# Graph network kernel: column numbers in PSUM for the merges, 30 batches fetched early, scores from folded source products

## The reference, cut to what matters

```
# layer 1 (relations), last step: sum the edge messages by destination, and add them to x
out = segment_sum(msg, dst);  x = x + out
# layer 2: this, twice (first on h = relu(layernorm(x)), then on its own output h1)
q = h @ wq + bq;  k = h @ wk + bk;  v = h @ wv + bv;  e = edge_attr @ we
score = sum(q[dst] * (k[src] + e), -1) / 8
alpha = softmax of score over the edges of one dst
out   = segment_sum(alpha[:, None] * (v[src] + e), dst) + h @ ws + bs
```

## Time and profile before

| | us |
|---|---|
| median of 3 runs | 6880.25 (6879.4 to 6884.29) |
| the profiled execution, its own time | 6867.82 |
| its span in the profile | 6865.4 |
| busy: PE, DVE, ACT, POOL | 4521.3, 4547.4, 1784.2, 3994.9 |
| stretch of rew, from its first hot to its last sum | 2401 to 2744 |
| at1s | 2779 to 3606 |
| at1w | 3642 to 3984 |
| at2s | 4016 to 4826 |
| at2w | 4867 to 5205 |

### The profile page before, as it was taken

The page is one execution under the profiler, slowest core; times in us unless marked ns, Lnnn a source line. Parts: engine busy times, 40 slices in busy tenths (PEclk is TensorE's granted clock), DMA queues, the critical chain, the costliest instruction groups (busy, mean ns, idle before and its releaser), DMA issues. The chain is left out here.

```text
span 6865.4 us, 102108 instructions
## 1 busy us (share of the span) xinstructions
PE 4521.3 (66%) x31726; PEld 4063.2 (59%) x31726; DVE 4547.4 (66%) x5826; ACT 1784.2 (26%) x2462; POOL 3994.9 (58%) x3348
## 2 busy tenths in 40 slices
PE   6665345770188788466766857777587856875897
PEld 3454335660177787466665856766587755764675
DVE  7898553225677788699989833333887965772458
ACT  5543112330044344233323411111343420000001
POOL 0397765771277678777765877775000027757756
PEclk9766668995598999688778979999899978997999
DMA  6498766668855477333335844444477861221109
GB/s 234 108 275 257 154 149 140 141 133 321 339 174 166 136 243 251 78 96 99 101 84 184 265 125 136 131 131 125 149 254 281 312 244 41 56 91 50 14 11 299
DMA packets 865606, 1128.70 MB, mean 164 GB/s; under 512 B 591583, under 2 KB 604276, under 8 KB 864060
## 3 DMA queue, kind: packets, MB, share of 16 engines
q1 hardware_dynamic: 409660, 807.13, 35.3%
q10 hardware_dynamic: 311296, 226.11, 10.8%
q0 software_dynamic: 144256, 90.12, 9.0%
HBM read 633.88 MB, written 495.44 MB: 164 GB/s over the span
## 5 line engine op out<-in xcount | busy, mean ns | idle before, releaser
L895 POOL DMA_INDIRECT gc_msgs<-t,src_rows x784 | 754.4, 962 | 1131.5 <-POOLq L148 837.3
L2005 PEld LDWEIGHTS gc_ring<-gc_msgs,gc_hot 128*128 128x128 f32 x4736 | 621.6, 208 | 310.4 <-issue 303.6
L2005 PE MATMUL gc_ring<-gc_msgs,gc_hot 128*128 x4736 | 648.8, 295 | 234.1 <-SPq L1964 233.0
L949 POOL DMA_INDIRECT acc<-de_sums,de_put x392 | 607.5, 1550 | 307.7 <-issue 146.6
L895 POOL DMA_INDIRECT edge_rows<-x,dst_rows x392 | 508.4, 1297 | 164.9 <-issue 117.1
L895 POOL DMA_INDIRECT edge_rows<-h,dst_rows x392 | 479.5, 1223 | 210.5 <-issue 117.3
L895 POOL DMA_INDIRECT re_rows<-x,src_rows x392 | 406.2, 1036 | 125.3 <-issue 124.7
L895 POOL DMA_INDIRECT at1s_ends<-x,src_rows x392 | 395.6, 1009 | 128.8 <-issue 119.2
L895 POOL DMA_INDIRECT at2s_ends<-h,src_rows x392 | 372.3, 950 | 134.7 <-issue 118.2
L1477 PE MATMUL re_psR<-w_rel,re_own 128*128 128x128 f32 x3136 | 396.9, 292 | 70.9 <-DVE re_own L1414 70.4
L1477 PEld LDWEIGHTS re_psR<-w_rel,re_own 128*128 128x128 f32 x3136 | 389.6, 208 | 80.1 <-issue 77.1
(11 more groups left out here) (491 smaller groups left out, 11718.9 us busy)
## 6 DMA issues: line engine op xcount, KB each, us to landing
rew_win<-x SPq DMA_DIRECT2D x74, 544.0 KB, 4.8
at1w_win<-g SPq DMA_DIRECT2D x74, 544.0 KB
at2w_win<-g SPq DMA_DIRECT2D x74, 544.0 KB, 4.1
de_win<-t ACTq DMA_DIRECT2D x74, 512.0 KB, 4.6
de_near<-same SPq DMA_DIRECT2D x74, 512.0 KB, 5.0
x<-rew_win SPq DMA_DIRECT2D x74, 512.0 KB
h<-at1w_win SPq DMA_DIRECT2D x74, 512.0 KB
h<-at2w_win SPq DMA_DIRECT2D x74, 512.0 KB, 2.9
```

The source lines that it names most:

```text
L895: nc.gpsimd.indirect_dma_start(buf[:, t * width:(t + 1) * width], None, table, bass.IndirectOffsetOnAxis(ap=rows[:, t:t + 1], axis=0)).the ...
L949: nc.gpsimd.indirect_dma_start(g.acc0[j % LANES], bass.IndirectOffsetOnAxis(ap=put[:, j:j + 1], axis=0), sums[:, j * D:(j + 1) * D], None, ...
L2005: done = nc.tensor.matmul(ring[:, bass.ds(to[n], SLOT)], hot[k][:, n, :], each_group(msgs[:, bass.ds(of[n], MID)], SLOT // MID), start=Fal ...
```

## The change

Four edits.

1. In the merges VectorE reads the column numbers from a copy in PSUM (`fixed`, one bank). For that bank the two output buffers, `ring[0:2048]` and `ring[1536:3584]`, now overlap in one bank: the last four steps' slots of a block. The odd block's slots run backwards. ScalarE clears 12 slots of a block early (`clear`) and the four shared ones (`clear_shared`) only once the block before has been summed out; TensorE waits for that ahead of its product 12.
2. `AHEAD` is 30: destination rows of batches 24 to 29 move, 48 gathers each, from at1s into rew and from at2s into at1w. The score stages make 544 gathers.
3. Scores: k and v of an edge and the score's form in the query weights come from one product of width 258 (`psU`, four banks): 128 columns for (k+e) wq^T, 128 for v+e, 2 for bq.(k+e). The biases come in by a row of ones under the transposed attributes. The folded weights are made once per stage (`lay_out` and the first six products of TensorE). Gone are the transposes `psD`, the copy `hdT`, q, k, three bias additions and, in at1s, the scaling of the destination rows by the layernorm's root (eight numbers per partition are scaled instead). `score` is now `dot` (VectorE: max, times, sum), `keep` (ScalarE: v+e and the two columns out of `psU`) and a small sum.
4. The own products of at2s take both weight tables as one of 256 columns (`own_w`): half as many instructions, equal columns.

The diff, cut; in merges the addresses of the products differ to match, and in `setup` a column table for them:

```diff
-AHEAD = 24
+AHEAD = 30
...
+                link(v.tensor_scalar(ahead[:, :], edge[:, :], edge[:, 0:1], None, ALU.subtract))
+                link(v.tensor_tensor(lift[:, :], ahead[:, :], at[:, :], ALU.subtract))
+                link(v.scalar_tensor_tensor(lift[:, :], lift[:, :], odd[:, :], at[:, :], ALU.mult, ALU.add))
+                link(v.tensor_scalar(g.steps[:, 2 * S:3 * S], lift[:, :], float(SLOT), None, ALU.mult))
...
-        ps = [r.ps(f"ps{k}", [P, S * SLOT]) for k in range(2)]
+        ring, fixed = r.ps("ring", [P, RING]), r.ps("fixed", [P, 512])
+        SHARED = 3 * 512
+        MOST = SHARED // SLOT
+        upper = ring[:, SHARED:SHARED + S * SLOT]
+        slots = [grouped(ring[:, 0:S * SLOT], SLOT), grouped(upper, SLOT)[:, ::-1, :]]
...
+                    to = grouped(local[m % 2][:, :], SLOT) if m % 2 else grouped(local[m % 2][:, :], SLOT)[:, ::-1, :]
+                    nc.scalar.activation(to[:, :, 0:D], grouped(msgs[:, bass.ds(first, S * D)], D), ACT.Copy).then_inc(copied, 1)
+
+                def width(m):
+                    return SLOT if m < 2 else D if counts is None else D + 1
 
                 def clear(m):
                     if m >= 2:
                         act.wait_ge(added, m - 1)
-                    width = SLOT if m < 2 else D if counts is None else D + 1
-                    nc.scalar.activation(grouped(ps[m % 2][:, :], SLOT)[:, :, 0:width], each_group(blank[:, 0:width], S), ACT.Copy).then_inc(zeroed, 1)
+                    nc.scalar.activation(slots[m % 2][:, 0:MOST, 0:width(m)], each_group(blank[:, 0:width(m)], MOST), ACT.Copy).then_inc(zeroed, 1)
+
+                def clear_shared(m):
+                    if m >= 1:
+                        act.wait_ge(added, m)
+                    nc.scalar.activation(slots[m % 2][:, MOST:S, 0:width(m)], each_group(blank[:, 0:width(m)], S - MOST), ACT.Copy).then_inc(zeroed_shared, 1)
...
+                copy(0)
+                clear(0)
                 for m in range(BLOCKS):
-                    copy(m)
-                    clear(m)
+                    if m + 1 < BLOCKS:
+                        copy(m + 1)
+                    clear_shared(m)
+                    if m + 1 < BLOCKS:
+                        clear(m + 1)
...
+                        if n == MOST:
+                            pe.wait_ge(zeroed_shared, m + 1)
+                        back = slice((S - 1 - n) * SLOT, S * SLOT)
+                        to, of = (upper[:, back], local[k][:, :]) if k else (ring[:, 0:S * SLOT], local[k][:, back])
+                        done = nc.tensor.matmul(to[:, bass.ds(at[n], SLOT)], hot[k][:, n, :], of[:, bass.ds(at[n], SLOT)],
...
+                v.tensor_copy(fixed[:, 0:P], g.across[:, :]).then_inc(fixed_made, 1)
...
-                        v.tensor_tensor(hot[m % 2][:, :, :], each_group(g.across[:, :], S), spread(g.steep[:, m * S:(m + 1) * S], P),
+                        v.tensor_tensor(hot[m % 2][:, :, :], each_group(fixed[:, 0:P], S), spread(g.steep[:, m * S:(m + 1) * S], P),
...
-                eng.wait_ge(ahead[b.slot], 16 * B * b.nth)
...
-                        nc.tensor.transpose(psD[:, k * P:(k + 1) * P], values[:, b.number * W + k * P:b.number * W + (k + 1) * P], g.ident[:, :])
-                    transpose_pairs(nc, psE, ea[s % 2], g.ident, B // 4)
-                    transpose_pairs(nc, psX, x[:, 0:W], g.ident, B // 2).then_inc(turned, 1)
+                        nc.tensor.transpose(psE[0:D, k * P:(k + 1) * P], ea[s % 2][:, k * D:(k + 1) * D], g.ident[:, :])
+                    transpose_pairs(nc, psX, xd[s % 2][:, 0:W], g.ident, B // 2).then_inc(turned, 1)
...
-                    times(nc, psQ, hdT[s % 2], wq, B // 2)
-                    for to, w in ((psK, wk), (psV, wv)):
-                        for h in range(2):
-                            nc.tensor.matmul(to[:, h * 256:(h + 1) * 256], eaT[s % 2][:, h * P:(h + 1) * P], we[:, :], start=True, stop=False,
-                                             skip_group_check=True)
-                            for k in range(2):
-                                j = 2 * h + k
-                                last = nc.tensor.matmul(to[:, j * P:(j + 1) * P], hsT[s % 2][:, j * P:(j + 1) * P], w[:, :], start=False, stop=(k == 1),
-                                                        skip_group_check=True)
+                    for j in range(B // 2):
+                        nc.tensor.matmul(psU[:, j, 0:PUT], eaT[s % 2][0:D + 1, j * P:(j + 1) * P], from_attr[:, :], start=True, stop=False,
+                                         skip_group_check=True)
+                        last = nc.tensor.matmul(psU[:, j, 0:PUT], hsT[s % 2][:, j * P:(j + 1) * P], from_src[:, :], start=False, stop=True,
+                                                skip_group_check=True)
...
-                            times(nc, psY, xT[s % 2][:, h * W:(h + 1) * W], g.w[dense[n][0]], B // 2).then_inc(piece, 1)
+                            times(nc, psY, xT[s % 2][:, m * EACH * P:(m + 1) * EACH * P], own_w, EACH).then_inc(piece, 1)
...
-                    nc.scalar.activation(hdT[s % 2][:, :], psD[:, :], ACT.Relu)
-                    nc.scalar.activation(eaT[s % 2][:, :], psE[:, 0:B * DE], ACT.Copy)
+                    nc.scalar.activation(eaT[s % 2][0:D, :], psE[0:D, :], ACT.Copy)
...
+                def keep(b):
+                    act.wait_ge(dotted, b.number + 1)
+                    nc.scalar.activation(grouped(far(b), P), psU[:, :, P:2 * P], ACT.Copy)
+                    nc.scalar.activation(grouped(scores[:, bass.ds(b.number * B, B)], 2), psU[:, :, 2 * P:PUT], ACT.Copy).then_inc(used, 1)
                 if normalise:
-                    pipeline(act, order=[(1, root), (1, turn), (0, square), (4, nothing)], slots=SLOTS)
+                    written_out(order=[(1, root), (2, keep), (1, turn), (0, square)], slots=SLOTS)
                 else:
-                    pipeline(act, order=[(1, turn), (4, nothing)], slots=SLOTS)
+                    written_out(order=[(2, keep), (1, turn)], slots=SLOTS)
...
+                def lay_out():
+                    v = nc.vector
+                    v.tensor_copy(key_rows[0:D, :], we[0:D, 0:P])
+                    v.tensor_copy(grouped(key_rows[D:D + 1, :], D), each_group(bk[D:D + 1, :], 2))
+                    v.tensor_copy(grouped(query_bias[:, :], D), each_group(bq[:, :], 2)).then_inc(laid, 1)
...
+                    v.tensor_copy(from_src[:, P:2 * P], wv[:, :])
+                    v.tensor_copy(from_attr[0:D, P:2 * P], we[0:D, 0:P])
+                    v.tensor_copy(grouped(from_attr[D:D + 1, P:2 * P], D), each_group(bv[D:D + 1, :], 2))
...
+                    for to, ps in ((from_src[:, :], psX[:, :]), (from_attr[:, :], psY[0:D + 1, :])):
+                        v.tensor_copy(to[:, 0:P], ps[:, 0:P])
+                        last = v.tensor_copy(to[:, 2 * P:PUT], ps[:, P:P + 2])
+                    last.then_inc(weights_made, 1)
...
-                    nc.vector.tensor_tensor(grouped(far(b), D), grouped(far(b), D), spread(root[:, 0, B:J], D), ALU.mult)
...
+                def dot(b):
+                    if not normalise:
+                        dve.wait_ge(ahead[b.slot], 16 * B * b.nth)
+                    dve.wait_ge(product, b.number + 1)
+                    nc.vector.scalar_tensor_tensor(grouped(dots[:, :], P), grouped(far(b), P), 0.0, psU[:, :, 0:P], ALU.max, ALU.mult).then_inc(dotted, 1)
+                    dve.wait_ge(dotted, b.number + 1)
+                    link(nc.vector.tensor_reduce(found[:, :], grouped(dots[:, :], D), AXX, ALU.add))
+                    if normalise:
+                        link(nc.vector.tensor_tensor(found[:, :], found[:, :], sd[b.slot % 2][:, 0, B:J], ALU.mult))
+
                 def score(b):
-                    s = b.slot
-                    dve.wait_ge(product, b.number + 1)
-                    nc.vector.tensor_tensor(grouped(q[:, :], D), grouped(psQ[:, :], D), each_group(bq[:, :], B), ALU.add)
-                    nc.vector.tensor_tensor(grouped(values[:, bass.ds(b.number * W, W)], D), grouped(psV[:, :], D), each_group(bv[:, :], B), ALU.add)
-                    nc.vector.tensor_tensor(grouped(k_[:, :], D), grouped(psK[:, :], D), each_group(bk[:, :], B), ALU.add).then_inc(used, 1)
+                    at = scores[:, bass.ds(b.number * B, B)]
                     dve.wait_ge(used, b.number + 1)
-                    link(nc.vector.tensor_tensor(q[:, :], q[:, :], k_[:, :], ALU.mult))
-                    link(nc.vector.tensor_reduce(scores[:, bass.ds(b.number * B, B)], grouped(q[:, :], D), AXX, ALU.add))
+                    link(nc.vector.tensor_tensor(at, at, found[:, :], ALU.add))
...
-                    pipeline(dve, order=[(1, variance), (1, scale), (2, score), (2, take(0)), (0, centre), (2, take(1))], slots=SLOTS)
+                    pipeline(dve, order=[(1, variance), (1, scale), (2, dot), (2, take(0)), (2, score), (0, centre), (2, take(1))], slots=SLOTS)
                 else:
```

(4 more changed lines are left out.)

77 lines of the change are left out of this document (54 added, 23 removed).

## The result

The changed kernel takes 6710.81 us (median of 4 runs, 6700.49 to 6723.98), beside 6881.99 for the kernel before (4 runs, 6879.4 to 6884.29): 0.9758 of the time, 95% interval 0.9746 to 0.9771, or 166 us less by that ratio and 171 by the two medians (162 were forecast, and the time given as 6718). Run again later on another chip it came to 0.9741 [0.9725, 0.9758]. The span of the profiled execution is 6709.1 us, that of before 6865.4.

The account below looks back on a forecast made before the run. Both merges end by GpSimd's slow gathers; at1s ties VectorE and GpSimd, at2s is TensorE's chain plus GpSimd's double batches. -26 - 31 - 30 - 79 + 4 = -162 gives 6718 us for the median; 60% for 6695 to 6745.

Parts of the forecast that it names:

- The bound of the merges: Merges rew and at1w: GpSimd's gathers end them late; with the operand in PSUM, 240 gathers take 300 us.
- rew to at1s: Way from merge rew into score stage at1s: ends by ScalarE instead of by gathers, -26 us (bounds -20 and -28).
- at1w to at2s: Way from merge at1w into score stage at2s: first gather at 3986 in place of 4016, -30 us (bound -22).
- I am wrong if merges grow: Sign against the forecast: the three merges were to stay at 343, 342 and 338 us within 3.
- at1s: First score stage: VectorE's round 16.0 to 13.9 us and fewer gathers, -31 us; lower bound of the gain -4.
- the 1.0 us of delay per batch: In at1s: about 1 us added to GpSimd's gathers per batch beside VectorE's two-operand work; 37 x 1.0 in the sum.
- at2s: Second score stage: TensorE's round 14.69 to 12.5 us and fewer gathers, -79 us (bounds -37 and -103).
- the reading of 16.1 us a round before: In at2s, kernel before: mean round above 14.69 us because of granted clock 0.90 and GpSimd's 30 us double batches.
- The lower bound of -37: In at2s: the gain if a round keeps 14.69 us and only GpSimd's double batches are fewer.
- The third rival: Score stages keep their round pace because the new chain is as long: at1s -4, at2s -37, 6787 us; 15%.
- The fourth: Rival: no GpSimd delay in at1s (-12), 11.4 us rounds in at2s (-12), 6695; at GpSimd's free pace 6665; 13%.
- The small things: `lay_out` opening each score stage, column copies, semaphores and contention of 48 more gathers per merge: +4 us (0 to +10).

Follow-up runs that it names:

- The operand's run: Kernel after with the comparison `hot` reading its column numbers from SBUF again, all else kept; 6862.83 us, 0.9991 of the kernel before.
- the runs with 30 and with 49 batches: Kernel before with only the number of destination batches fetched early raised, to 30 (6978.65 us, 1.0164 of before) and to 49 (7351.29 us, 1.0699).

## Why the prediction held, and where it didn't

**The bound of the merges: right.** GpSimd ended them, the operand made it late, and with it in PSUM 240 gathers take 300 us. The operand's run shows the cause. The section of the Trainium skill that I set against the trace ("SBUF — State Buffer", § Who interferes with whom) is borne out in its rule that a VectorE instruction with two SBUF inputs contends with a GpSimd instruction that reads SBUF. Its inference that such instructions do not hold up descriptor generation doesn't carry over to these gathers: one of 0.95 us became one of 2.66. Whether the reading of the row numbers or the generation itself was held up, no run tells.

**rew to at1s: right but for 4 us.** From rew's first hot to at1s's first gather it is -22 and -25 in the two profiles, where -26 stood. ScalarE's last work ended at 2756.10 and not at 2749.70, as rew itself had grown by 5.7 in the first; the exit behind it was 1.8 us and not 4. **at1w to at2s:** -26 and -28 for -30, with an exit of 5.1 for 4.6 + 0.6; the growth of at1w by 2 to 4 us is the rest. The forecast took at1w's first `hot` at 3642 and the merges at 343, 342 and 338 us; by the view by tile that `hot` starts at 3645.0, and from first hot to last sum they were 341.4, 335.7 and 331.3. "I am wrong if merges grow" came true in small: they grew by 5.7, 4.3 and 1.8 us, in the second run by 2.5, 2.0 and 3.0, which the sum had at nothing.

**at1s: the mechanism right, its size within what the stage scatters.** -23 and -35 with the way behind it, for -31. Forecast 764 us to the last sum; 769.8 and 761.5. The term that moves is the 1.0 us of delay per batch: the 448 gathers to the end of the double batches took 605 us in the first profile, 45 more than 448 x 1.25, or 1.2 a batch.

**at2s: right in sign, 10 us short, with a wrong step in it.** -90 and -89 for -79. The round is 11.59 us, where my sum gave 11.4 to 11.7 and I took 12.5 "with dips of the clock": that carried over the clock of before to a round that no longer had it. Batch 37's first transpose starts 571.6 us into the stage, where 571.5 stood; the 11 rounds behind it take 129.3 us in place of 137, and the way behind the last turn is 5.0 and 3.1 us shorter in place of 1: these two are the 10 us. The step that failed outright is the reading of 16.1 us a round before. I put it down to the clock and to GpSimd's double batches; the runs with 30 and with 49 batches leave 784.6 and 780.0 us of 786.2, so GpSimd's part was 2 to 6 us, and the rest was the clock, as the single rounds show. The lower bound of -37 "if only the doubles are fewer" was therefore no bound: it would have been -2. The waits of the trace said so: behind the stage's start TensorE waited 1.6 us for gathers (49.7 - 48.1). I had read the waits and still shared the blame.

**The third rival** (the score rounds keep their pace) did not come: with `keep` on ScalarE in the chain, none of TensorE's waits in at2s names it: it stands behind the dot and beside the own pieces. **The fourth** came halfway, in at2s only.

**The small things:** +4 forecast. at2w and what is behind it are 4.9 and 4.3 us longer, start and setup +0.7 and -0.5. `lay_out` lies under the first gathers: VectorE still waits 6.06 us for them behind it.

What stays open is the growth of the merges with undelayed gathers, 2 to 2.5 us each: more transfers in the same time is the likely reason, and no run took them apart from the rest.

## What to carry to other kernels

Before an engine's queue is called slow, look for what the other engines run beside its late instructions: here one operand of one VectorE instruction, moved to PSUM at no cost to itself, shortened the gathers beside it, from 1433 to 946 ns in the mean of rew's 240. Value the parts of a change for the limit that stands after the others: fetching earlier cost 113 us alone and brought some 70 with the other parts. And before a limit is shared between two causes, take one away whole: a stage whose length hardly moves when a queue loses a third of its work (786.2 to 780.0 us from 592 gathers to 392) was not bound by it.

## What the runs showed of the hardware

- A gather that starts beside a VectorE comparison with both operands in SBUF ends 0.82 us behind it, in the kernel before and in the experiment alike (0.81 to 0.83 in 142 of 145, and in 142 of 143); with one operand in PSUM it takes 0.95 us as when alone. Both forms of the comparison take 2.28 us for 2048 elements.
- The granted clock of TensorE was 0.98 over a stage in which it was busy 78% in 2360 instructions, and 0.92 over the older form of it, busy 72% in 3994. A busier engine was not the slower one. In the older form each round holds a wait of up to 3.6 us, in the new one none above 1.6 once gathers don't hold it up, and where they did (up to 4.7 us) the new form had 0.89 as well. The lower clock went with the longer waits; no run changed the waits alone.
- Half as many TensorE instructions with twice the columns each saved 0.03 us on 1.16.
